# Mamba layer with routed experts on one core: expert tiles every 3.25 steps instead of 3.5, token gathers from step 197 and 4.5 steps apart, one product with C moved back to GpSimd

## The chip, the core and the metric

The kernel runs on one core of a Trainium2 chip. The metric is the time of one execution on the device, in microseconds. A core has five engines that run side by side, each through its own list of instructions in order: PE (TensorE, matmuls), DVE (VectorE), ACT (ScalarE), POOL (GpSimd) and SP (SyncE, here the queue from which nearly all DMAs are issued). They wait for one another by semaphores only. An instruction that waits holds back all that stands behind it on its engine.

## What is computed

The input is x of 8 batches x 512 tokens x 128. Each token is normalized; the result goes into two branches whose outputs are added to x. One branch is a bidirectional Mamba layer (a forward and a backward pass), the other a mixture of 8 experts of which each token takes the one with the highest router logit. Cut to what matters:

```
xn = layernorm(x)
# Mamba, once forward and once on the reversed sequence, per batch
xz = layernorm(xn)*g+b  @ in_w.T ; xi, z = split(xz)         # 256 channels each
xi = silu(conv4(xi) + conv_b)
dt, B, C = split(xi @ x_w.T)                                 # 8, 16, 16
delta = softplus(dt @ dt_w.T + dt_b) ; A = -exp(A_log)
h_t = h_{t-1} * exp(delta_t * A) + (delta_t * xi_t) * B_t    # 256 channels x 16 states
y_t = sum over states of h_t * C_t                           # "the product with C", then the sum
y = (y + xi * D) * silu(z) ; out = y @ out_w.T
attn = concat(out_f, out_b) @ combine_w.T + combine_b + xn
# experts
e = argmax(xn @ router_w.T)
ffn = (silu(xn @ gate_w[e].T) * (xn @ up_w[e].T)) @ down_w[e].T
result = x + attn + ffn
```

## The kernel before

**Units and steps.** A unit is one batch in one direction, so there are 16. One unit has 256 channels x 16 states x 512 tokens, cut into 16 steps of 128 rows x 1024 (two states of 32 channels). The whole kernel is a loop over 256 such steps, m = 0 to 255 (`LAST` = 256), written out on every engine: each engine's program runs `for m in range(STEPS)` and puts down, at each m, what is due there by tables and small functions of m.

**What a step is.** PE spreads delta*xi over the state rows for a pair of steps (`spread_du`, L600, put down at odd m for the pair m+1, m+2; it waits for the scan of step m-2, since the PSUM tile `in_b` has two halves). DVE multiplies by B (`du_B`, L1195, both steps of the pair), then scans (`scan`, L1212 or L1214). ACT makes the decays dA two steps ahead (L1002). POOL multiplies the scanned states `hs` by C, in place (L1435, 128x1024). Some of these products are done by DVE instead (`times_C`, L1221): those whose step stands in `C_ON_DVE`. PE then sums the states into the PSUM tile `y` (`sum_states`, L634).

**The ring of `hs`.** `hs` has NH = 13 buffers. Steps 8g to 8g+7 are a group; its even steps are summed at PE's step 8g+12 and its odd ones at 8g+13. The scan of step m needs the sum of the group and parity of step m-13. So the scan of step 8g+13 waits for the first sum of group g, and that waits for POOL's product of step 8g+6.

**Fronts.** The projections of the next unit (`in_proj` L561, `x_proj` L584, `dt_proj` L593, `z_proj` L575, and what ACT makes of them) stand some 16 to 4 steps ahead of it, in a ping-pong of PE and ACT over one PSUM bank. POOL makes delta and delta*xi (L1376, L1381), twice for each unit.

**Experts.** The routing sorts the tokens by expert into 39 tiles of 128 (`NTILE`). Tile n starts at step F0 + 7n//2 (`tiles_at`, F0 = 56): its loads stand there, gate matmuls (L784) 8 steps later, down and up matmuls (L802, L807) 10 steps later, ACT's SiLU and copies (L1066, L1071, L1088, L1090, L1094, L1098, with table loads L1011) 9 and 11 steps later, POOL's product gate*up (L1425) 11 or 12. Expert outputs go to HBM.

**Gathers.** When all tiles are out, the outputs are gathered back into token order, a batch at a time, in the order 0, 1, 2, 3, 6, 4, 5, 7 (`gather_step`, from step G0 = 206, 4 steps apart). At gather step + 2 POOL issues four indirect DMAs (L1408, or L1411 for the last two batches), ahead of the product with C of that step. For batches 0 to 5 PE adds them to the attention output at gather step + 7 (`final_mm`, L702 and, behind a wait for the gather, L704), ACT copies the sum (L1116), SP stores it. Batches 6 and 7 are added elsewhere (`experts_mm`, L691, at steps 236 and 257). At steps 233 to 237 PE also makes the output of batch 6 (L678, L685, L710). At step `FOUR` = 244 the preparation of the last sum begins (L643, L649).

Steps of the units' fronts, of the outputs and of the end (`front_step`, `out_step`, `LAST`) are fixed; the tables decide only the order of instructions on each engine.

## Time and profile before

| | before |
|---|---|
| runs, us | 912.49, 917.79, 912.06; median 912.49 |
| profiled execution, us | 918.05, of which the span is 916.1 |
| PE, DVE, ACT, POOL busy | 81%, 96%, 76%, 87% of the span |
| granted TensorE clock, mean | 0.886 of full speed |
| chain that ended last | POOL 15%, issue 9%, PE 5%, ACT 4%, DVE 1% |

The span is from the first to the last instruction of the profiled execution. Busy time of an engine is the time in which it executes something. An idle time is put down to the engine and line that ended it.
### The profile page before, as it was taken

How to read it: one execution, taken by the hardware profiler on the slowest of the kernel's cores; microseconds unless marked ns; L12 is line 12 of the kernel's file. 1: busy time of each engine (PE TensorE's matmuls, PEld its weight loads, DVE VectorE, ACT ScalarE, POOL GpSimd, SP SyncE). 2: the span in 40 equal slices, each digit the busy share in tenths (PEclk: the TensorE clock that was granted, in tenths of full speed). 3: DMA queues.
4: the chain of work that ended last, by engine and by line, in shares of the span. 5: the costliest groups of instructions: out<-in, count | busy, mean ns of one | idle time of the engine just before them, and what ended most of it. 6: DMA issues, size and time to landing. Idle time of an engine off the chain costs nothing. (4 is left out here: it accounts for less than half of the span.)

```text
span 916.1 us, 10763 instructions
## 1 busy us (share of the span) xinstructions
PE 743.8 (81%) x3045; PEld 331.8 (36%) x3045; DVE 882.0 (96%) x633; ACT 696.9 (76%) x1185; POOL 801.0 (87%) x450
## 2 busy tenths in 40 slices
PE   8889866877489978889798987989979879788376
PEld 4434321331034534354443533435333432223022
DVE  5999999999899999999899999999999999999987
ACT  4898965746379889888889889997979976575540
POOL 1578787999999999898898988999798999999995
PEclk9969889787799989989799998989999897979689
DMA  7795443235355555645455636555553534553300
GB/s 216 200 287 122 129 103 103 87 101 136 92 140 178 134 188 146 189 106 127 156 130 178 158 78 195 139 167 148 174 141 99 141 87 153 118 173 73 91 0 12
DMA packets 87371, 123.52 MB, mean 135 GB/s; under 512 B 7945, under 2 KB 58634, under 8 KB 83346
## 3 DMA queue, kind: packets, MB, share of 16 engines
q1 hardware_dynamic: 85266, 118.65, 46.9%
q0 software_dynamic: 2048, 4.20, 1.5%
q8 instruction: 25, 0.41, 0.2%
q14 instruction: 32, 0.26, 0.1%
HBM read 75.50 MB, written 14.29 MB: 98 GB/s over the span
## 5 line engine op out<-in xcount | busy, mean ns | idle before, releaser
L1435 POOL TENSOR_TENSOR hs<-hs,C_rep 128x1024 f32<-128x1024 f32 x250 | 585.7, 2362 | 46.7 <-DVE hs L1214 26.1
L1002 ACT ACTIVATE dA<-delta_rep,A_sb 128x511 f32<-128x511 f32 x512 | 335.4, 717 | 22.8 <-DMA delta_rep<-tmpA 18.6
L1195 DVE TENSOR_TENSOR in_b<-in_b,B_rep 128x1024 f32<-128x1024 f32 x256 | 300.2, 1217 | 12.2 <-PE in_b L600 10.5
L1214 DVE TENSOR_TENSOR_SCAN hs<-dA,in_b 128x1024 f32<-128x1024 f32 x128 | 285.5, 2269 | 5.1 <-PE y L634 5.1
L1212 DVE TENSOR_TENSOR_SCAN hs<-dA,in_b 128x1024 f32<-128x1024 f32 x128 | 285.3, 2269 | 1.0 <-PE y L634 1.0
L600 PE MATMUL in_b<-du,cst 128*128 128x512 f32 x256 | 159.1, 707 | 68.5 <-DVE hs L1214 49.6
L634 PE MATMUL y<-hs,cst 128*32 128x512 f32 x1016 | 136.3, 655 | 22.3 <-POOL hs L1435 22.3
L561 PE MATMUL front<-xpad,w_in 128*128 128x512 f32 x248 | 117.6, 609 | 8.5 <-ACT xi L931 6.4
L1011 ACT ACT_TABLE_LOAD x71 | 91.1, 1283 | 11.6 <-PE moe L784 7.1
L600 PEld LDWEIGHTS in_b<-du,cst 128*128 128x128 f32 x256 | 47.5, 216 | 142.7 <-issue 139.8
L561 PEld LDWEIGHTS front<-xpad,w_in 128*128 128x128 f32 x248 | 46.1, 195 | 64.0 <-issue 48.7
L634 PEld LDWEIGHTS y<-hs,cst 128*32 128x32 f32 x1016 | 28.3, 116 | 105.1 <-issue 67.2
L575 PE MATMUL front<-xpad,w_in 128*128 128x512 f32 x62 | 45.6, 828 | 17.1 <-ACT tmpB L967 11.5
L1376 POOL TENSOR_TENSOR tmpA<-tmpA,tmpB 128x512 f32<-128x512 f32 x31 | 39.5, 1273 | 13.7 <-ACT tmpB L977 13.7
L593 PE MATMUL front<-tmpB,w_dt 8*128 8x512 f32 x62 | 41.3, 750 | 9.2 <-ACT tmpB L953 7.1
L625 PE MATMUL y<-xi,diag_D 128*128 128x512 f32 x62 | 42.4, 772 | 7.8 <-ACT yg L985 6.5
L784 PEld LDWEIGHTS moe<-xsT,gu_w 128*128 128x128 f32 x234 | 33.0, 203 | 36.1 <-issue 36.1
L784 PE MATMUL moe<-xsT,gu_w 128*128 128x128 f32 x234 | 36.1, 294 | 9.7 <-ACT ys L1071 7.2
L1418 POOL TENSOR_TENSOR yg<-yg,zs 128x512 f32<-128x512 f32 x28 | 35.6, 1270 | 9.5 <-ACT yg L985 9.4
L802 PEld LDWEIGHTS moe<-dn_w,th_f 128*128 128x128 f32 x234 | 33.2, 202 | 26.3 <-issue 19.2
L584 PE MATMUL front<-xi,w_x 128*40 128x512 f32 x64 | 35.5, 683 | 7.9 <-ACT xi L944 7.9
L1381 POOL TENSOR_TENSOR du<-tmpA,xi 128x512 f32<-128x512 f32 x31 | 39.5, 1273 | 2.4
(158 smaller groups left out, 813.7 us busy)
## 6 DMA issues: line engine op xcount, KB each, us to landing
delta_rep<-tmpA SPq DMA_DIRECT2D x126, 256.0 KB, 3.9
C_rep<-dbc_scratch SPq DMA_DIRECT2D x16, 1024.0 KB, 7.1
B_rep<-dbc_scratch SPq DMA_DIRECT2D x15, 1024.0 KB, 5.1
gu_w<-in_gate_up SPq DMA_DIRECT2D x39, 384.0 KB, 3.7
dn_w<-in_down SPq DMA_DIRECT2D x39, 192.0 KB, 2.6
xs<-sorted_tokens SPq DMA_DIRECT2D x39, 64.0 KB, 3.8
sorted_ffn<-ys SPq DMA_DIRECT2D x39, 64.0 KB, 2.5
sorted_tokens<-up_f SPq DMA_DIRECT2D x9, 256.0 KB, 4.6
```

Source lines behind the costliest of these rows:

```text
L561: i = e.matmul((M if v == 0 and h else F)[:, :], w_in[:, d, k, h * P:(h + 1) * P], xpad[:, at:at + L], start=(k == 0), stop=(k == NTAP - 1))
L575: e.matmul((M if v == 0 and h else F)[:, :], w_in[:, d, NTAP, h * P:(h + 1) * P], xpad[:, 3:3 + L], start=True, stop=True).then_inc(pe_z, 1)
L600: e.matmul(in_b[:, 2 + 2 * (j % 2), :], spread(j), du[:, du_slot(v, j // 4), :], start=True, stop=True).then_inc(pe_du, 1)
L625: e.matmul(Y[:, :], diag_D[:, 2 * (u % 2) + h, :], xi[:, u % 2, h, :], start=True, stop=False, skip_group_check=True).then_inc(pe_skip, 1)
L634: i = e.matmul(Y[c * DD:(c + 1) * DD, :], sel, hs[:, (m + 2 * c + rh) % NH, r * L:(r + 1) * L], start=False, stop=(rh == 1 and r == RH - 1 ...
L784: i = e.matmul(M[:, c * P:(c + 1) * P], gu_w[:, w, 0, c * P:(c + 1) * P], xsT[:, n % 2, :], start=True, stop=True)
L1002: i = e.activation(dA[:, m % NA, r * L + 1:(r + 1) * L], src, ACT.Exp, scale=A_sb[:, d, 2 * p + jj, RH * rh + r:RH * rh + r + 1])
L1011: e.preload_act_table_set(name)
L1195: e.tensor_tensor(to, in_b[:, 2 + 2 * odd, :].unsqueeze(1).broadcast_to([P, RH, L]), by, ALU.mult).then_inc(dve_mult, 1)
L1212: e.tensor_tensor_scan(to, a[:, 0:n], b, 0.0, ALU.mult, ALU.add).then_inc(dve_scan, 1)
L1214: e.tensor_tensor_scan(to[:, ::-1], a[:, 1:n + 1][:, ::-1], b[:, ::-1], 0.0, ALU.mult, ALU.add).then_inc(dve_scan, 1)
L1435: e.tensor_tensor(hs[:, m % NH, :], hs[:, m % NH, :], C_rep[:, u % 2, RH * rh:RH * rh + RH, :].rearrange("p r t -> p (r t)"), ALU.mult).th ...
```

## The change

Three sets of numbers change and no instruction is new.

- Tile n starts at F0 + 13n//4, so every 3.25 steps. The last tile's start moves from step 189 to 179, its last copy on ACT from 207 to 197.
- The first gather step is 197 and they are 4.5 steps apart: 197, 201, 206, 210, 215, 219, 224, 228 in place of 206, 210, 214, 218, 222, 226, 230, 234. POOL's issues are two steps later each, at 199, 203, 208, 212, 217, 221, 226, 230. `FOUR` is still 244, written in another way.
- The product with C of step 180 is POOL's again. Steps 41, 56, 217, 226 and 255 stay with DVE.

```diff
-C_ON_DVE = (41, 56, 180, 217, 226, LAST - 1)
+C_ON_DVE = (41, 56, 217, 226, LAST - 1)
...
-G0 = F0 + 7 * NTILE // 2 + 14
+G0 = F0 + 13 * NTILE // 4 + 15
...
-    return [n for n in range(NTILE + more) if F0 + 7 * n // 2 + k == m]
+    return [n for n in range(NTILE + more) if F0 + 13 * n // 4 + k == m]
...
-    return G0 + 4 * GATHER_ORDER.index(b)
+    return G0 + 9 * GATHER_ORDER.index(b) // 2
```

**DVE, step 180** (L1195 multiplies by B, L1214 scans, L1221 is the product with C). This is the only difference on DVE:

```order
 L1195 TENSOR_TENSOR in_b<-in_b,B_rep 128x2x512
 L1214 SCALAR_TENSOR_TENSOR hs<-dA,in_b 128x1024 x2
-L1221 TENSOR_TENSOR hs<-hs,C_rep 128x1024
 L1195 TENSOR_TENSOR in_b<-in_b,B_rep 128x1024 x2
 L1214 SCALAR_TENSOR_TENSOR hs<-dA,in_b 128x1024 x2
```

One product has gone, between the scans of steps 180 and 181 and the products with B of steps 182 and 183.

**POOL, the last gathers.** L1435 is the product with C, L1418 a gate of the unit's output, L1376 and L1381 delta and delta*xi, L1408 and L1411 the four gathers of a batch. Before, from the gather of batch 4 (step 228) to that of batch 7 (step 236):

```order
L1408 DMA gu_w<-sorted_ffn,pos_u 128x128 x4
L1435 TENSOR_TENSOR hs<-hs,C_rep 128x1024 x2
L1418 TENSOR_TENSOR yg<-yg,zs 128x512
L1435 TENSOR_TENSOR hs<-hs,C_rep 128x1024 x2
L1408 DMA gu_w<-sorted_ffn,pos_u 128x128 x4
L1376 TENSOR_TENSOR tmpA<-tmpA,tmpB 128x512
L1381 TENSOR_TENSOR du<-tmpA,xi 128x512
L1435 TENSOR_TENSOR hs<-hs,C_rep 128x1024 x2
L1376 TENSOR_TENSOR tmpA<-tmpA,tmpB 128x512
L1381 TENSOR_TENSOR du<-tmpA,xi 128x512
L1435 TENSOR_TENSOR hs<-hs,C_rep 128x1024 x2
L1411 DMA attn_in<-sorted_ffn,pos_u 128x128 x4
```

After the change, from the gather of batch 4 (step 221) to the product of step 233:

```order
L1408 DMA gu_w<-sorted_ffn,pos_u 128x128 x4
L1435 TENSOR_TENSOR hs<-hs,C_rep 128x1024
L1418 TENSOR_TENSOR yg<-yg,zs 128x512
L1435 TENSOR_TENSOR hs<-hs,C_rep 128x1024 x4
L1408 DMA gu_w<-sorted_ffn,pos_u 128x128 x4
L1435 TENSOR_TENSOR hs<-hs,C_rep 128x1024 x3
L1411 DMA attn_in<-sorted_ffn,pos_u 128x128 x4
L1418 TENSOR_TENSOR yg<-yg,zs 128x512
L1435 TENSOR_TENSOR hs<-hs,C_rep 128x1024 x2
L1376 TENSOR_TENSOR tmpA<-tmpA,tmpB 128x512
L1381 TENSOR_TENSOR du<-tmpA,xi 128x512
L1435 TENSOR_TENSOR hs<-hs,C_rep 128x1024 x2
```

All gathers stand ahead of the product of step 230 now, where batch 5's and batch 7's used to stand behind it. The two deltas of the last unit keep their steps, 232 and 234.

**PE, steps 224 to 229.** L561 is `in_proj` of the last unit, L600 `spread_du`, L702 and L704 `final_mm`, L634 the sum over states, L584 `x_proj`. Before:

```order
L561 MATMUL front<-xpad,w_in 128x512 x4
L600 MATMUL in_b<-du,cst 128x512
L702 MATMUL moe<-attn_in,cst 128x512
L704 MATMUL moe<-gu_w,cst 128x512
L561 MATMUL front<-xpad,w_in 128x512 x4
L600 MATMUL in_b<-du,cst 128x512
L634 MATMUL y<-hs,cst 32x512 x8
```

After the change:

```order
L561 MATMUL front<-xpad,w_in 128x512 x4
L600 MATMUL in_b<-du,cst 128x512
L561 MATMUL front<-xpad,w_in 128x512 x2
L702 MATMUL moe<-attn_in,cst 128x512
L704 MATMUL moe<-gu_w,cst 128x512
L561 MATMUL front<-xpad,w_in 128x512 x2
L600 MATMUL in_b<-du,cst 128x512
L634 MATMUL y<-hs,cst 32x512 x8
```

The final product that stands here is batch 4's (step 226), seven steps after its gather step 219; before it was batch 3's (step 225). Behind it stand two matmuls of `in_proj` and the spread for steps 228 and 229. The final product of batch 5 moves from step 237 to 231.

## Rows read from the trace of the kernel before

**Rows 1.** The page, busy time of each engine (share of the span, instructions).
```profile
PE 743.8 (81%) x3045; PEld 331.8 (36%) x3045; DVE 882.0 (96%) x633; ACT 696.9 (76%) x1185; POOL 801.0 (87%) x450
```

**Rows 2.** Groups by line, DVE: count | busy us, mean ns | idle before, ended by.
```profile
L1195 DVE TENSOR_TENSOR in_b<-in_b,B_rep 128x1024 f32<-128x1024 f32 x256 | 300.2, 1217 | 12.2 <-PE in_b L600 10.5 <-DMA B_rep<-dbc_scratch 1.6
L1214 DVE TENSOR_TENSOR_SCAN hs<-dA,in_b 128x1024 f32<-128x1024 f32 x128 | 285.5, 2269 | 5.1 <-PE y L634 5.1
L1221 DVE TENSOR_TENSOR hs<-hs,C_rep 128x1024 f32<-128x1024 f32 x6 | 9.2, 1529 | 0.1
```

**Rows 3.** Waits of DVE: us in total, times, longest us.
```profile
DVE in_b L1195 <- PE in_b L600: 10.5, 7, 3.7
DVE hs L1214 <- PE y L634: 5.1, 2, 2.8
```

**Rows 4.** Timeline of DVE, steps 207 and 238 to 246.
```profile
737.56 2.26 DVE L1212 TENSOR_TENSOR_SCAN hs<-dA,in_b 128x1024 f32<-128x1024 f32 x1
...
844.63 4.46 DVE L1212 TENSOR_TENSOR_SCAN hs<-dA,in_b 128x1024 f32<-128x1024 f32 x2 [0.89 <-PE y L634]
...
855.63 2.34 DVE L1195 TENSOR_TENSOR in_b<-in_b,B_rep 128x1024 f32<-128x1024 f32 x2
...
862.25 2.34 DVE L1195 TENSOR_TENSOR in_b<-in_b,B_rep 128x1024 f32<-128x1024 f32 x2
...
869.04 2.29 DVE L1214 TENSOR_TENSOR_SCAN hs<-dA,in_b 128x1024 f32<-128x1024 f32 x1 [2.27 <-PE y L634]
875.02 2.36 DVE L1195 TENSOR_TENSOR in_b<-in_b,B_rep 128x1024 f32<-128x1024 f32 x2 [3.69 <-PE in_b L600]
```

**Rows 5.** Timeline of POOL, the first gather and the end of the last.
```profile
742.54 1.01 POOL L1408 DMA_INDIRECT gu_w<-sorted_ffn,pos_u  x1 [0.16 <-issue]
...
747.33 9.29 POOL L1435 TENSOR_TENSOR hs<-hs,C_rep 128x1024 f32<-128x1024 f32 x4
...
837.76 1.28 POOL L1376 TENSOR_TENSOR tmpA<-tmpA,tmpB 128x512 f32<-128x512 f32 x1
...
862.95 18.52 POOL L1435 TENSOR_TENSOR hs<-hs,C_rep 128x1024 f32<-128x1024 f32 x8
```

**Rows 6.** Timeline of PE, steps 224 to 245.
```profile
789.36 3.60 PE L561 MATMUL front<-xpad,w_in 128*128 128x512 f32 x8
...
838.18 1.95 PE L710 MATMUL front<-w_out,yg 128*128 128x128 f32 x16
...
842.64 1.92 PE L634 MATMUL y<-hs,cst 128*32 128x512 f32 x16
...
855.86 2.04 PE L600 MATMUL in_b<-du,cst 128*128 128x512 f32 x2 [5.52 <-DVE hs L1214]
865.33 3.64 PE L634 MATMUL y<-hs,cst 128*32 128x512 f32 x16 [7.43 <-POOL hs L1435]
```

**Rows 7.** The line of the gathers, issue to landing.
```profile
DMA to landing us min/median/max: 2.5/2.6/3.8
```

**Rows 8.** Timeline of DVE at two of its products with C.
```profile
174.93 3.05 DVE L1221 TENSOR_TENSOR hs<-hs,C_rep 128x1024 f32<-128x1024 f32 x1
...
652.58 1.20 DVE L1221 TENSOR_TENSOR hs<-hs,C_rep 128x1024 f32<-128x1024 f32 x1
```

**Rows 9.** Timeline of POOL beside these two.
```profile
174.53 2.36 POOL L1435 TENSOR_TENSOR hs<-hs,C_rep 128x1024 f32<-128x1024 f32 x1
...
652.75 3.26 POOL L1435 TENSOR_TENSOR hs<-hs,C_rep 128x1024 f32<-128x1024 f32 x1 [4.10 <-DVE hs L1214]
```

**Rows 10.** Timeline of DVE, first and last of four waits among the tiles.
```profile
342.89 2.36 DVE L1195 TENSOR_TENSOR in_b<-in_b,B_rep 128x1024 f32<-128x1024 f32 x2 [0.83 <-PE in_b L600]
...
539.96 2.36 DVE L1195 TENSOR_TENSOR in_b<-in_b,B_rep 128x1024 f32<-128x1024 f32 x2 [1.50 <-PE in_b L600]
```

**Rows 11.** Windows: us, PE, PEld, DVE, ACT, POOL busy, clock, DMA share, GB/s.
```profile
275.00:545.00 270.00, 236.54 (x1117) 118.97 (x1109) 264.50 (x161) 238.89 (x411) 249.52 (x137) 0.92 0.53 148
...
735.00:840.00 105.00, 83.91 (x265) 30.37 (x264) 104.97 (x65) 70.15 (x111) 97.11 (x63) 0.87 0.43 118
```

More of the change, by code:

```diff
@@ L105, in out_step @@
     return s0 + (8, 9, 18, 21, 4, 22, 25, 17)[k]
-FOUR = gather_step(GATHER_ORDER[-1]) + 10
+FOUR = LAST - 12
 STEPS = max(LAST + 6, out_step(NB - 1, 6) + 1, gather_step(NB - 1) + 10)
```

## The prediction, made before the changed kernel ran

> **What bounds the kernel now.** I read the busy times first: DVE is busy for 96% of the span, no other engine for more than 87% [rows 1]. Then DVE's groups: 256 products with B take 300.2 us, the 128 scans of L1214 285.5 us and those of L1212, 128 too, as much; that is 871 of its 882 us, and ahead of them it hardly waits [rows 2]. So the time is the steps of DVE, plus what DVE waits. A pair of steps takes 862.25 - 855.63 = 6.62 us where nothing disturbs it [rows 4], 3.31 a step. What can be gained is DVE's own work and its waits. These I took from the list of waits and looked up in the timeline: 10.5 us for the spread of PE and 5.1 us for PE's sums at L1214 [rows 3].
>
> They fall into two places. Four waits for the spread, 5.35 us together, lie among the expert tiles, the first of 0.83 us at 342.89 and the last of 1.50 us at 539.96 [rows 10]. Three lie at the end, ahead of steps 238, 245 and 246: 0.89 + 2.27 + 3.69 = 6.85 us [rows 4].
>
> The end is POOL's doing. The product of step 207 ends at 742.54 - 0.16 = 742.38, which is 2.56 us after its scan (737.56 + 2.26 = 739.82) [rows 4, 5]. The product of step 238 ends at 862.95 + 2.32 = 865.27, 18.4 us after its scan (846.90). I call this distance the lag. PE stands ready and starts the sum at 865.33, after 7.43 us of waiting for POOL [rows 6]. By the ring of 13 buffers the scan of step 245 needs that sum, and the spread for step 246 stands behind it, so DVE goes on at 875.02 only, 9.7 us after POOL's product.
>
> POOL's own prices: a product with C 18.52 / 8 = 2.32 us, the four gathers of a batch 747.33 - 742.38 = 4.95 us, a delta, a delta*xi or a gate (all 128x512) 1.28 us [rows 5]. From step 208 to 238 it has 29 products, 8 gathers, 8 deltas and 4 gates: 67.3 + 39.6 + 10.2 + 5.1 = 122.2 us; the trace has 122.9. In that time DVE needs 31 steps and two products, some 105 us. That is how the lag grows.
>
> **The change, part by part.**
>
> *Product of step 180.* DVE loses one instruction of 1.20 us at 652.58 [rows 8], 1.1 us without the overlap with the next. POOL gets it where it had idled for 4.10 us (ahead of 652.75) [rows 9], so it costs POOL nothing that shows. If that cover were gone, the lag would be 2.3 us longer there, against some 18 that the ring bears. **-1.1 us.** The row beside it shows more: POOL's product that started 0.17 us after DVE's took 3.26 instead of 2.36 us [rows 9], and DVE's product at 174.93, which started 0.40 us after one of POOL's, took 3.05 instead of 1.20 us [rows 8]. The Trainium skill says this (SBUF — State Buffer, Who interferes with whom): a VectorE instruction with both inputs in SBUF and a GpSimd one that reads SBUF exclude each other, whoever starts first has the port to its end. By that rule POOL pays 2.35 - 0.9 = 1.4 us for the product that it gets back; the trace agrees, with 0.9 us.
>
> *The gathers.* They start 9 steps earlier, so the lag starts to grow from step 199. I add the jobs up, e(m) being the end of scan m:
> - To product 221: 22 products, 6 gathers, 8 deltas, 2 gates: 51.0 + 29.7 + 10.2 + 2.6 = 93.5 us. DVE from e(198) to e(221): 11 pairs, 2.19 and one product, 76.1 us. Lag 2.5 + 17.4 = 19.9, and 0.6 more if this sum is short by as much as that of before: 20.5 us.
> - To product 230: 69.6 + 39.6 + 10.2 + 5.1 = 124.5 against 16 pairs and two products, 108.2. Lag 19.6 us.
> - To product 238: 88.2 + 39.6 + 15.4 + 6.4 = 149.6 against 134.7. Lag 18.3 us.
>
> So the lag at step 238, which made the waits of before, goes from 19.3 (18.4 without DVE's 0.89 us wait) to 18.3 only, and it is near 20 from step 221 on. Two new places come under it:
> - *Steps 226 to 228.* The last gather of batch 4 is issued about 1.0 us before the product of step 221 starts and lands 2.6 us later [rows 7]: e(221) + 20.5 - 2.35 - 1.0 + 2.6 = e(221) + 19.8. PE's final product of batch 4 waits for it, and behind it stand half of `in_proj` and the spread for step 228. DVE wants that at e(221) + 19.9 + 1.1 = 21.0. In PE's fast rows (a 128x512 matmul 0.45 us a pass, 3.60 / 8) the chain takes 0.9 + 1.8 + 0.9 = 3.6 us, in slow ones (2.04 for x2) 7.5 us [rows 6]. It is late by 2.4 or 6.3 us.
> - *Steps 236 to 238.* The sum that needs product 230 starts at e(230) + 19.6. Behind it stand the batch 6 experts' product, two output products and the spread for step 238, due at 22.05. Fast: 1.92 + 0.9 + 1.95 + 0.9 = 5.7, late by 3.2. Slow: 3.64 + 2.0 + 3.9 + 2.0 = 11.5, late by 9.1.
> - *Steps 244 to 246*, as before: 18.3 + 9.7 - 22.05 = 5.9 us late at the pace of before, 1.1 at twice that pace.
>
> Late amounts don't add: each wait of DVE lets POOL catch up by as much. What counts is the largest. Checked on before: 19.3 + 9.7 - 22.05 = 6.9 us, and the trace has 6.85. So the end costs between 3.2 and 9.1 us. The granted clock there was 0.87 up to 840, and the sum after 7.43 us of waiting ran at half speed, 3.64 instead of 1.92 us [rows 6, 11]. The new waits are as long (PE could take batch 4's final product some 11 us before its gather lands), so I take the slow end: 8.5 us. Against 6.85: **+1.65 us.** It is not a gain because the same 40 us of gathers go through POOL within steps that leave it less than 1 us a step.
>
> *Tiles every 3.25 steps.* The same 39 tiles, closer by 3.5 / 3.25 = 1.077 and over 10 steps earlier. In 275 to 545 PE is busy for 236.5 and ACT for 238.9 of 270 us [rows 11]; a wait of DVE comes where a tile's work falls among the front's ping-pong of PE and ACT. The four waits make 5.35 us. In proportion they become 5.8: **+0.4 us**, with both ends open: none at all (-5.35) or twice as much (+5.35), since their places are reshuffled. The cover of the first gather (its tiles stored in time) keeps its distance of two steps.
>
> **The sum**, against the profiled execution: 918.05 - 1.1 + 1.65 + 0.4 = 919.0 us. The median of the runs is 912.49, 5.56 below the profiled one, so I expect **913.4 us**, about the same.
>
> **The rivals.**
> - *The waits at the end shrink.* If PE stays fast, the end costs 3.2 instead of 6.85 us: 913.4 - (8.5 - 3.2) = 908.1. For it: nearly all of PE's rows around 790 to 843 are fast. Against it: the waits grow longer, and 865.33 was slow after one.
> - *The product's price alone shows.* The end and the tiles stay as they are: 912.49 - 1.1 = 911.4. For it: two of the three terms are small against their bounds.
> - *Tiles collide.* The waits among the tiles double: 913.4 + 5.0 = 918.4.
> - *DVE's products wait for POOL.* Before, the products of steps 217 and 226 met POOL at gathers. With a lag of 15 to 20 us POOL is never idle there, and each may meet one of POOL's products. As at 174.93, each is then 1.85 us longer [rows 8, 9]; I let this vanish in the waits that follow, but if it came on top it would be 913.4 + 3.7 = 917.1. This is the port rule of the page named above turned against the change.
> - *Slower by more than 1%: the waits add up.* PE has 21 us of idle time in the 105 us up to 840 [rows 11] and must now wait for the gathers of batches 1 to 5 as well, with the front of the last units behind. If it can't catch up between two waits, the three late amounts add: 6.3 + 9.1 + 5.9 = 21.3 instead of 6.85, less the 1.65 already counted: 913.4 + 12.8 = 926.2. It decides from a total of 16.7 us of DVE waits at the end on (6.85 + 9.1 + 1.1 - 0.4), where 912.49 is passed by 1%.
>
> **How the numbers follow.** Forecast 0.48 (own range 911 to 917), shrinking waits 0.24, product alone 0.08, tiles 0.08, port 0.06, adding waits 0.06. The range runs from the shrunken waits, 908, to the tiles' collision with a slower end, 920. A measurement of this kernel can tell about 1% (9 us) from no change. More than 9 us faster would need the end's and the tiles' waits all gone as well as the product (13.3 us in all); I give it 0.02. Slower by over 1% is the last rival and a little of two others: 0.07. The rest is 0.91.
>
> **What the profile after would show.** Right: DVE's L1221 five times; POOL's first gather near 712 us; POOL's lag near 20 us from step 221 to 236; PE waiting for gathers at L704 (no such wait before); DVE's waits at the end ahead of steps 228, 238 and 246, 5 to 9 us together; among the tiles 4 to 8 us. Wrong: if POOL's lag stays below 16 us, my prices for it are; if DVE waits less than 4 us at the end, PE's pace is; if the waits exceed 16 us, that they relieve each other is; if L1221 has rows near 3 us at steps 217 and 226, the port matters.

## The result: 2.5% slower, and the profile after

| | before | after |
|---|---|---|
| runs | median 913.3 us (6 runs, 912.06 to 917.79) | median 936.83 us (6 runs, 936.08 to 939.48) |
| ratio of the medians | | 1.0249, interval 1.022 to 1.0277 |
| profiled execution | 918.05 us, span 916.1 | 937.19 us, span 935.2 |
| granted clock, mean | 0.886 | 0.885 |
| DVE's idle time among the tiles (250 to 715 us) | 5.6 us | 18.3 us |
| DVE's products with C at steps 217 and 226 | 1.22 + 1.20 us | 10.67 + 2.56 us |
| DVE's idle time at the end of the loop | 6.85 us | 2.8 us |

I had forecast 913.4 us, within 908 to 920. The change is slower by 23.5 us in the medians, which is outside the range and on the other side of the 1% bound.

DVE is busy for 892.9 us, 11 more than before [rows 1], though it has one instruction less. These are the engines' busy times and the products with B on the page of the kernel after:

```profile
PE 749.7 (80%) x3045; PEld 337.9 (36%) x3045; DVE 892.9 (95%) x632; ACT 697.0 (75%) x1185; POOL 803.3 (86%) x451
L1195 DVE TENSOR_TENSOR in_b<-in_b,B_rep 128x1024 f32<-128x1024 f32 x256 | 300.1, 1217 | 15.9 <-PE in_b L600 15.7
```

The products with B take what they took before [rows 2], and so do the scans. The added busy time is in the line of DVE's products with C (count, shortest / median / longest in ns), where the longest was about 3 us before [rows 8]:

```profile
L1221 DVE TENSOR_TENSOR hs<-hs,C_rep x5: 1197/2561/10666, 174.0 to 927.3; 128x1024 f32<-128x1024 f32 x5
```

DVE's timeline after shows where it is (start, length, ..., in brackets the idle time ahead). The product of step 217 takes 10.67 us and that of step 226 2.56:

```profile
785.22 10.67 DVE L1221 TENSOR_TENSOR hs<-hs,C_rep 128x1024 f32<-128x1024 f32 x1
...
828.91 2.56 DVE L1221 TENSOR_TENSOR hs<-hs,C_rep 128x1024 f32<-128x1024 f32 x1
...
863.94 2.29 DVE L1212 TENSOR_TENSOR_SCAN hs<-dA,in_b 128x1024 f32<-128x1024 f32 x1 [1.37 <-PE y L634]
...
867.61 2.36 DVE L1195 TENSOR_TENSOR in_b<-in_b,B_rep 128x1024 f32<-128x1024 f32 x2 [1.38 <-PE in_b L600]
```

The last two rows are all that DVE waits at the end, 2.75 us. POOL's timeline over the same time says what stands beside the long product:

```profile
781.97 4.67 POOL L1435 TENSOR_TENSOR hs<-hs,C_rep 128x1024 f32<-128x1024 f32 x2
786.59 1.27 POOL L1418 TENSOR_TENSOR yg<-yg,zs 128x512 f32<-128x512 f32 x1
787.81 6.98 POOL L1435 TENSOR_TENSOR hs<-hs,C_rep 128x1024 f32<-128x1024 f32 x3
794.95 1.79 POOL L1411 DMA_INDIRECT xn<-sorted_ffn,pos_u  x1 [0.16 <-issue]
```

When DVE's product starts at 785.22, POOL is in the second of two products. It goes on with a gate and three more, each right behind the one before. They end at 787.81 + 6.98 = 794.79. DVE's product ends at 785.22 + 10.67 = 795.89, 1.10 us later, which is its own length. So it lasted 9.4 us longer than its work because POOL left no gap. It is counted as busy. Beside the length of its row, only the chain that ended last shows it, with no engine as its cause:

```profile
785.36 10.45 issue
```

The waits of DVE after, in 250 to 715 us (us in total, times, longest):

```profile
DVE in_b L1195 <- PE in_b L600: 11.6, 10, 2.9
DVE hs L1212 <- PE y L634: 4.7, 3, 2.2
DVE hs L1212 <- ACT dA L1002: 0.9, 1, 0.9
DVE hs L1214 <- ACT dA L1002: 0.6, 2, 0.3
DVE hs L1214 <- PE y L634: 0.5, 1, 0.5
```

That is 18.3 us in 17 waits. Before there were four waits of 5.35 us for the spread [rows 10] and one of 0.2 us for PE's sums, 5.6 us. Several of the runs below have the same program up to 715 us, but for the product of step 180, so their profiled executions say how much such a total moves from one execution to the next. Before's tables of tiles are in e3, e8 and e11 too: 3.7, 5.1 and 3.5 us. The changed tables are in e1, e2 and e4 too: 14.9, 24.8 and 19.9 us. The two groups stay well apart, but one total is good to some 5 us either way.

**The account between the two profiled executions:** tiles 18.3 - 5.6 = +12.7; the two products 13.23 - 2.42 = +10.8; the end of the loop 2.8 - 6.85 = -4.05; the product of step 180 -1.1. The sum is +18.4 us, and 937.19 - 918.05 = +19.1 us was measured. Between the medians the difference is 4.4 us larger, because the profiled execution of before lies 4.75 us above the median of its runs and that of after 0.4 us above its own.

### The profile page after: what moved, and what is told of

Same layout as the page of the kernel before. It is cut to its first block and busy times, and to the rows that moved or that the text cites. A ratio compares the mean times of both kernels' runs of the same rounds, so it can differ in the third digit from the quotient of the medians.

```text
span 935.2 us, 10763 instructions
## 1 busy us (share of the span) xinstructions
PE 749.7 (80%) x3045; PEld 337.9 (36%) x3045; DVE 892.9 (95%) x632; ACT 697.0 (75%) x1185; POOL 803.3 (86%) x451
## 5 line engine op out<-in xcount | busy, mean ns | idle before, releaser
L1435 POOL TENSOR_TENSOR hs<-hs,C_rep 128x1024 f32<-128x1024 f32 x251 | 587.4, 2359 | 58.2 <-DVE hs L1214 39.6
L1195 DVE TENSOR_TENSOR in_b<-in_b,B_rep 128x1024 f32<-128x1024 f32 x256 | 300.1, 1217 | 15.9 <-PE in_b L600 15.7
L1214 DVE TENSOR_TENSOR_SCAN hs<-dA,in_b 128x1024 f32<-128x1024 f32 x128 | 285.7, 2270 | 4.2 <-PE y L634 3.6
L600 PE MATMUL in_b<-du,cst 128*128 128x512 f32 x256 | 156.1, 695 | 70.2 <-DVE hs L1214 45.3
L634 PE MATMUL y<-hs,cst 128*32 128x512 f32 x1016 | 137.7, 661 | 17.3 <-POOL hs L1435 17.3
L561 PE MATMUL front<-xpad,w_in 128*128 128x512 f32 x248 | 121.4, 624 | 9.3 <-ACT xi L931 7.2
L600 PEld LDWEIGHTS in_b<-du,cst 128*128 128x128 f32 x256 | 47.5, 215 | 145.0 <-issue 145.0
L561 PEld LDWEIGHTS front<-xpad,w_in 128*128 128x128 f32 x248 | 47.2, 200 | 66.8 <-issue 51.0
L634 PEld LDWEIGHTS y<-hs,cst 128*32 128x32 f32 x1016 | 28.6, 117 | 99.4 <-issue 68.1
L575 PE MATMUL front<-xpad,w_in 128*128 128x512 f32 x62 | 45.3, 822 | 18.7 <-ACT zs L937 11.4
L784 PE MATMUL moe<-xsT,gu_w 128*128 128x128 f32 x234 | 38.7, 308 | 20.1 <-ACT ys L1071 14.0
L1376 POOL TENSOR_TENSOR tmpA<-tmpA,tmpB 128x512 f32<-128x512 f32 x31 | 39.6, 1276 | 17.3 <-ACT tmpB L977 17.2
L784 PEld LDWEIGHTS moe<-xsT,gu_w 128*128 128x128 f32 x234 | 34.1, 213 | 46.4 <-issue 46.3
L593 PE MATMUL front<-tmpB,w_dt 8*128 8x512 f32 x62 | 39.4, 718 | 8.7 <-ACT tmpB L953 4.5
L1418 POOL TENSOR_TENSOR yg<-yg,zs 128x512 f32<-128x512 f32 x28 | 35.6, 1272 | 11.9 <-ACT yg L985 11.8
L802 PEld LDWEIGHTS moe<-dn_w,th_f 128*128 128x128 f32 x234 | 33.1, 203 | 33.5 <-issue 24.2
L802 PE MATMUL moe<-dn_w,th_f 128*128 128x128 f32 x234 | 36.1, 294 | 7.5 <-POOL th_f L1425 5.3
L1381 POOL TENSOR_TENSOR du<-tmpA,xi 128x512 f32<-128x512 f32 x31 | 39.5, 1273 | 2.4
```

The costliest lines, as they stand in the source:

```text
L561: i = e.matmul((M if v == 0 and h else F)[:, :], w_in[:, d, k, h * P:(h + 1) * P], xpad[:, at:at + L], start=(k == 0), stop=(k == NTAP - 1))
L575: e.matmul((M if v == 0 and h else F)[:, :], w_in[:, d, NTAP, h * P:(h + 1) * P], xpad[:, 3:3 + L], start=True, stop=True).then_inc(pe_z, 1)
L600: e.matmul(in_b[:, 2 + 2 * (j % 2), :], spread(j), du[:, du_slot(v, j // 4), :], start=True, stop=True).then_inc(pe_du, 1)
L634: i = e.matmul(Y[c * DD:(c + 1) * DD, :], sel, hs[:, (m + 2 * c + rh) % NH, r * L:(r + 1) * L], start=False, stop=(rh == 1 and r == RH - 1 ...
L784: i = e.matmul(M[:, c * P:(c + 1) * P], gu_w[:, w, 0, c * P:(c + 1) * P], xsT[:, n % 2, :], start=True, stop=True)
L802: i = e.matmul(M[:, IFP:IFP + H], th_f[:, (n - 2) % 3, c * P:(c + 1) * P], dn_w[:, (n - 2) % ND, c, :], start=(c == 0), stop=(c == NCH - 1))
```

## The experiments

The kernel before was run again beside each group of experiments. Its medians were 911.86 us beside e1 to e4, 912.86 beside e5 to e8, 913.52 beside e9 and e10, and 914.02 beside e11. Two things need a cause: the 12.7 us among the tiles, and the long product.

### e1: the tiles alone

The kernel before with the tiles every 3.25 steps. Gathers and products stay.

```diff
-    return [n for n in range(NTILE + more) if F0 + 7 * n // 2 + k == m]
+    return [n for n in range(NTILE + more) if F0 + 13 * n // 4 + k == m]
```

> The kernel before with only the tile spacing changed: expert tiles every 3.25 steps; gathers stay at 206 and 4 steps apart, DVE keeps the product of step 180. In the changed kernel's trace DVE's waits between 270 and 705 us are 17.7 us, in the trace before 5.5. Theory tiles (the closer tiles alone make these waits): the same waits of 15 to 20 us here, and 10 to 15 us more than before in all, ratio 1.011 to 1.016; no DVE product with C longer than 1.3 us at step 217. Rival (the waits among the tiles come with the removed product of step 180 or with something else of the change): waits of 4 to 8 us, ratio within 0.997 to 1.004.

Measured: median 930.61 us (925.58 to 933.62), ratio 1.021, interval 1.0157 to 1.0262. The tiles alone bring 18.75 us in the medians, most of the change's 23.5. What is left, some 5 us, is for the gathers and the product of step 180 together; neither was run alone, and the intervals of the two ratios overlap. DVE's product of step 217 took 1.22 us here, so the gathers are needed for the long one. DVE's waits in 250 to 715 us, profiled execution of 925.58 us:

```profile
DVE in_b L1195 <- PE in_b L600: 9.6, 10, 2.2
DVE hs L1212 <- PE y L634: 3.2, 3, 2.6
```

With the three small groups (0.9 + 0.6 + 0.6) that is 14.9 us, 9.3 more than before. One wait followed back shows how they come about. First ACT's timeline in e1:

```profile
493.72 1.28 ACT L1011 ACT_TABLE_LOAD   x1
495.01 2.56 ACT L1002 ACTIVATE dA<-delta_rep,A_sb 128x511 f32<-128x511 f32 x4
...
498.88 0.28 ACT L1071 COPY ys<-moe 128x128 f32<-128x128 f32 x1
```

and then PE's:

```profile
499.41 0.91 PE L784 MATMUL moe<-xsT,gu_w 128*128 128x128 f32 x6 [3.63 <-ACT ys L1071]
...
502.18 2.08 PE L625 MATMUL y<-xi,diag_D 128*128 128x512 f32 x2
...
505.82 1.81 PE L600 MATMUL in_b<-du,cst 128*128 128x512 f32 x2
```

ACT copies the tile's output (`ys`) behind a table load, four exponentials and three more instructions. PE, whose next instruction is the tile's product, stands for 3.63 us. It comes back at half speed: 2.08 us for a 128x512 matmul of two passes, where the last one ahead of the wait took 1.02 (granted clock 1.00 in 495 to 499.4 us, 0.59 in 499.4 to 507.7). So the spread for the next step ends at 507.63, and DVE waits 0.71 us for it:

```profile
507.67 2.36 DVE L1195 TENSOR_TENSOR in_b<-in_b,B_rep 128x1024 f32<-128x1024 f32 x2 [0.71 <-PE in_b L600]
```

PE waited for this copy (L784 for L1071) ten times between 250 and 715 us, 13.7 us; before, seven times and 7.2 us. Its waits for weight loads went from 2.5 to 6.2 us and those for POOL's product for the tile (L802 for L1425) from none to 6.7 us.

### e2: the two products on POOL

The changed kernel with DVE's products of steps 217 and 226 given to POOL.

```diff
-C_ON_DVE = (41, 56, 217, 226, LAST - 1)
+C_ON_DVE = (41, 56, LAST - 1)
```

> The changed kernel, with DVE's products of steps 217 and 226 given to POOL too. In the changed kernel they take 10.67 and 2.56 us instead of 1.2. Theory port (DVE's product can't start while POOL runs products back to back, and waits until POOL issues a gather): both rows are gone and DVE runs on at 217, 13 us less there; but POOL has 4.7 us more work and isn't relieved by that wait, so its lag, which was 10.8 us at step 221, goes to 22 or more, and DVE waits at PE's sums and spreads from step 228 on for 9 to 16 us instead of 2.8. In all -6 to +1 us against the changed kernel: 931 to 938 us. Rival (the 10.67 us were a wait of that place in the program, for memory or for data, which any instruction there would have had): the next instruction, the product with B of step 218, is late by 9 us instead, and POOL's lag stays near 11 us.

Measured: median 938.34 us (933.04 to 942.83), ratio 1.0267, interval 1.0197 to 1.0338. This can't be told from the changed kernel. The long product is gone, and the lag comes in its place: product 221 ends 23.0 us behind its scan. DVE's waits in 715 to 930 us:

```profile
DVE in_b L1195 <- issue: 7.3, 1, 7.3
DVE in_b L1195 <- PE in_b L600: 5.6, 2, 4.1
```

With 0.3 us more for ACT that is 13.2 us instead of 2.8. The wait of 7.3 us, for which the profile names no one, lies ahead of step 234 (DVE goes on at 857.09). In PE's timeline the spread that it needs ends at 855.67 + 1.38 = 857.05, and ahead of that spread PE waits 7.43 us for the gather of batch 5 and comes back slow:

```profile
847.53 2.07 PE L704 MATMUL moe<-gu_w,cst 128*128 128x512 f32 x2 [7.43 <-DMA gu_w<-sorted_ffn,pos_u]
...
855.67 1.38 PE L600 MATMUL in_b<-du,cst 128*128 128x512 f32 x2
```

So the two products held DVE for 10.8 us longer than their work and saved 10.4 us of waits, because POOL caught up in the meantime: the standing by itself is hardly a net loss against giving the products to POOL. (The waits among the tiles, 24.8 us here, are the spread between executions named above.)

### e3: a DVE product beside a run of POOL's

The kernel before with one more product on DVE, at step 242, where POOL has products in a row and no gather.

```diff
-C_ON_DVE = (41, 56, 180, 217, 226, LAST - 1)
+C_ON_DVE = (41, 56, 180, 217, 226, 242, LAST - 1)
```

> The kernel before, with the product of step 242 given to DVE as well, in a stretch without gathers, where POOL runs products back to back (from 857 us on). Theory port: DVE's product starts near 862 us and ends only when POOL falls idle, which it does once it has made the products of 238 to 241 and 243 and must wait for the scan of step 244, near 875 us: a row of 10 to 14 us. The waits of 2.3 and 3.7 us at steps 245 and 246 vanish into it, so the kernel is 4 to 8 us slower than before. Rival (a DVE product waits for one POOL product at most, as at 174.93 in the trace before: 3.05 us): a row of 1.2 to 3.5 us, and the time within 3 us of before or below it, as POOL has one product less.

Measured: median 924.59 us (two runs, 922.88 and 926.29), ratio 1.0126, interval 1.0058 to 1.0195. DVE's row for it:

```profile
859.86 13.36 DVE L1221 TENSOR_TENSOR hs<-hs,C_rep 128x1024 f32<-128x1024 f32 x1
```

and POOL's:

```profile
859.32 1.27 POOL L1418 TENSOR_TENSOR yg<-yg,zs 128x512 f32<-128x512 f32 x1
860.54 11.60 POOL L1435 TENSOR_TENSOR hs<-hs,C_rep 128x1024 f32<-128x1024 f32 x5
877.76 4.66 POOL L1435 TENSOR_TENSOR hs<-hs,C_rep 128x1024 f32<-128x1024 f32 x2 [5.62 <-DVE hs L1214]
```

The product stands behind the rest of a gate and five products, six instructions of POOL. POOL goes idle at 872.14, and DVE's product ends at 873.22, 1.08 us later. That is 12.1 us of standing, and nothing but a gap on POOL ends it: a gather after the change, idleness here. DVE's waits of before at steps 245 and 246 (2.27 + 3.69 us [rows 4]) are gone, since POOL caught up. The kernel is made slower all the same: by 4.8 us between the profiled executions, within the 4 to 8 us expected, but by 12.7 us between the medians, which of two runs is a rough figure and outside it.

### e4: the two products at POOL's gathers

The changed kernel with DVE's products at steps 215 and 225, where by the lag POOL is issuing gathers.

```diff
-C_ON_DVE = (41, 56, 217, 226, LAST - 1)
+C_ON_DVE = (41, 56, 215, 225, LAST - 1)
```

> The changed kernel, with DVE's two products at steps 215 and 225 instead of 217 and 226, where POOL should be issuing the gathers of batches 3 and 4. Theory port: POOL issues gathers while DVE makes the product of 215, so that row is 1.2 to 1.5 us and the one of 225, at the edge of a gather, 1.2 to 3.5; POOL's lag at step 221 is 19 to 21 us instead of 10.8; DVE waits 4 to 9 us at the end instead of 2.8. In all 5 to 9 us less than the changed kernel: 928 to 932 us. Rival (long rows come with any product of DVE in that stretch): a row of 5 us or more again and 936 us.

Measured: median 932.02 us (928.25 to 936.98), ratio 1.0211, interval 1.0144 to 1.0277. DVE's timeline:

```profile
779.89 1.23 DVE L1221 TENSOR_TENSOR hs<-hs,C_rep 128x1024 f32<-128x1024 f32 x1
...
814.25 1.23 DVE L1221 TENSOR_TENSOR hs<-hs,C_rep 128x1024 f32<-128x1024 f32 x1
816.96 2.36 DVE L1195 TENSOR_TENSOR in_b<-in_b,B_rep 128x1024 f32<-128x1024 f32 x2 [1.48 <-PE in_b L600]
...
824.11 2.36 DVE L1195 TENSOR_TENSOR in_b<-in_b,B_rep 128x1024 f32<-128x1024 f32 x2 [0.43 <-PE in_b L600]
...
849.56 2.36 DVE L1195 TENSOR_TENSOR in_b<-in_b,B_rep 128x1024 f32<-128x1024 f32 x2 [5.49 <-PE in_b L600]
```

Against the changed kernel that is 4.8 us less, at the edge of the 5 to 9 us expected, and the intervals of the two ratios overlap. Between the profiled executions it is 4.8 us too: the two products give back 10.8 us, the waits at the end take 4.6 and those among the tiles 1.6.

Both products take 1.23 us, two steps and one step away from where they took 10.67 and 2.56. POOL pays for the second one with a gather that takes 1.75 instead of 0.95 us:

```profile
814.54 1.75 POOL L1408 DMA_INDIRECT gu_w<-sorted_ffn,pos_u  x1 [0.30 <-issue]
...
818.81 2.35 POOL L1435 TENSOR_TENSOR hs<-hs,C_rep 128x1024 f32<-128x1024 f32 x1
```

This last row is the product of step 221. It ends at 821.16, 20.2 us after its scan (which ends at 800.99); 20.5 us was forecast. PE's timeline has the two final products that wait for their gathers and then delay DVE, batch 4's and batch 5's:

```profile
820.37 1.12 PE L704 MATMUL moe<-gu_w,cst 128*128 128x512 f32 x2 [0.69 <-DMA gu_w<-sorted_ffn,pos_u]
...
840.11 2.07 PE L704 MATMUL moe<-gu_w,cst 128*128 128x512 f32 x2 [5.73 <-DMA gu_w<-sorted_ffn,pos_u]
```

Batch 4's starts at 820.37, where the prediction's sum gives 800.99 + 19.8 = 820.8. PE was fast, DVE had waited 1.48 us already at step 226, and what is left ahead of step 228 is 0.43 us. Batch 5's is a place that I hadn't reckoned: it makes the wait of 5.49 us ahead of step 234. Its gather took 6.78 us to land, in the chain that ended last:

```profile
833.28 6.78 DMA gu_w<-sorted_ffn,pos_u
```

where all gathers of before landed within 3.8 us [rows 7]. Of the stretch in which it was under way and of the one behind it the windows say this (us, busy PE, PEld, DVE, ACT, POOL, clock, DMA share, GB/s):

```profile
833.00:840.00 7.00, 1.38 (x4) 0.31 (x2) 7.00 (x6) 2.11 (x4) 6.71 (x4) 0.89 0.84 296
840.00:850.00 10.00, 9.70 (x12) 3.05 (x12) 4.51 (x3) 6.77 (x13) 8.91 (x8) 0.56 0.23 68
```

The DMA engines were busy for 84% of those 7 us; with the earlier gathers batch 5's now falls beside the broadcasts of B and C for the last unit. That these delay it is argued from the window, no run took them away. Behind PE's wait the clock is 0.56, near the lower of its levels, 0.5, and the matmul of two passes takes 2.07 us in place of 1.12. Together DVE waits 7.4 us at the end, where the prediction had 8.5 for the changed kernel.

### e5, e6, e7: the same tiles at other places

The kernel before; only the table of tile steps is changed. e5: 3.5 steps, all one step later. e6: 3.25 steps, one step later. e7: 3.5 steps with the gaps in the order 4, 3 in place of 3, 4. The gathers stay where they were.

```diff
 # e5 (e6: the same, and 13 * n // 4 in place of 7 * n // 2 for the tiles)
-F0 = R0 + 29
-G0 = F0 + 7 * NTILE // 2 + 14
+F0 = R0 + 30
+G0 = R0 + 29 + 7 * NTILE // 2 + 14
```

```diff
 # e7
-    return [n for n in range(NTILE + more) if F0 + 7 * n // 2 + k == m]
+    return [n for n in range(NTILE + more) if F0 + (7 * n + 1) // 2 + k == m]
```

> The kernel before with all expert tiles one step later, still every 3.5 steps; gathers as before. DVE's waits between 250 and 715 us are 5.5 us before and 14.9 us with tiles every 3.25 steps (e1_tiles). Theory density (more of the gaps between tiles are 3 steps, where PE's gate matmuls stand in the same step as ACT's copy that they wait for; 28 of 38 gaps at 3.25, 19 at 3.5): the shift changes nothing of it, waits of 4 to 8 us, time within 4 us of before. Theory place (what counts is where tiles fall within the 16 steps of a unit's front): waits move by 4 us or more, to 9 to 16 us, and the time goes up by 4 to 12 us.

> The kernel before with tiles every 3.25 steps and all of them one step later. Theory density: as e1_tiles, waits of 13 to 17 us among the tiles, 925 to 932 us. Theory place: waits differ from the 14.9 us of e1_tiles by 4 us or more, either way.

> The kernel before with tiles every 3.5 steps, but the gaps of 3 and 4 steps swapped: 4 from an even tile to the odd one behind it, 3 to the next even one. The number of gaps of 3 is as before (18 of 38). POOL's product of an even tile stands 11 steps behind the start of the odd tile, and PE's down matmuls of it 10 steps behind the start of the next even one: 2 steps instead of 3. Theory pool_product (PE's waits for POOL's product gate*up, 0 before and 5 to 7 us in the two kernels with 3.25, are a main part of the loss): these waits appear here, 5 us or more, and DVE's waits among the tiles go to 10 us or more. Theory density: DVE's waits 4 to 8 us, PE waits for POOL's product 3 us at most.

(Of the 38 gaps between tiles 29 are of three steps at 3.25, and 19 at 3.5, in e7 too; the texts above give 28 and 18.)

| tiles | median, us | ratio, interval | DVE's waits 250 to 715 us |
|---|---|---|---|
| before: 3.5 | 912.86 | | 5.6 |
| e5: 3.5, a step later | 930.86 | 1.0189, 1.0157 to 1.0221 | 16.7 |
| e7: 3.5, gaps swapped | 939.62 | 1.0293, 1.0273 to 1.0314 | 20.5 |
| e1: 3.25 | 930.61 | 1.021, 1.0157 to 1.0262 | 14.9 |
| e6: 3.25, a step later | 932.78 | 1.0221, 1.0198 to 1.0244 | 19.7 |

Density alone doesn't explain the loss: at 3.5 steps, a step later, the kernel is as slow as at 3.25 (e5's 18 us are more than the 4 to 12 that its own theory of place had). With the same gaps in another order it is the slowest of all. The tiles of the kernel before stand in a good place, and any of the four other tables costs 18 to 27 us. The last column is one execution for each table and can't rank the four slow ones: 14.9 to 24.8 us were seen with e1's table alone. The waits that open on PE differ from table to table. The largest group of PE's in e5, e6 and e7, each in 250 to 715 us:

```profile
PE moe L784 <- ACT ys L1071: 10.5, 8, 2.5
PE moe L784 <- DMA gu_w<-in_gate_up: 9.3, 5, 4.2
```

```profile
PE moe L784 <- ACT ys L1071: 26.8, 15, 4.6
```

```profile
PE moe L784 <- ACT ys L1071: 14.0, 7, 4.9
...
PE moe L802 <- POOL th_f L1425: 5.9, 4, 2.4
```

ACT's copy comes first in all three, with 10.5 to 26.8 us where before had 7.2. Next to it stand weight loads in e5 and POOL's product for the tile in e7, where the swap leaves it a step less. That product's wait came as e7's theory said, 5 us or more, but in e5 and e6 it is 1.4 and 1.5 us and the loss is there all the same, so it is no common cause.

### e9 and e10: less of ACT, less of PE

Both start from e1. Their expectations say what they leave out of the experts. e9 leaves out the tiles' SiLU and with it the change of ACT's function tables, 36 of 71 table loads. e10 keeps one of every three matmuls of the tiles' products.

```diff
 # e9
-                        table(SILU_SET)
-                        e.activation(th_f[:, n % 3, :], M[:, 0:IFP], ACT.Silu).then_inc(act_gate, 1)
+                        e.activation(th_f[:, n % 3, :], M[:, 0:IFP], ACT.Identity).then_inc(act_gate, 1)
...
-                        e.activation(t, t, ACT.Silu).then_inc(act_thf, 2)
+                        e.activation(t, t, ACT.Identity).then_inc(act_thf, 2)
```

```diff
 # e10
-                    for c in range(NCH):
+                    for c in range(1):
...
-                    for c in range(NCH if n >= 2 else 0):
+                    for c in range(1 if n >= 2 else 0):
...
-                    for c in range(NCH if n < NTILE else 0):
+                    for c in range(1 if n < NTILE else 0):
```

> The kernel with only the tiles every 3.25 steps (e1_tiles), with the SiLU of the expert tiles left out (a plain copy in its place), so that the tiles need no table loads on ACT: about 40 of its 71 loads of 1.28 us fall away, 1.3 us of some 3.1 us of ACT's work for a tile. The output of the experts is another. Theory ACT (PE is held up in its list by ACT's copies, which stand behind table loads and decays): DVE's waits between 250 and 715 us fall from 14.9 to below 5 us and PE's waits for ACT's copy ys fall from 13.7 to below 6 us; 908 to 918 us. Theory PE (the tiles' matmuls themselves leave PE no room): DVE's waits stay above 10 us.

> The same kernel (tiles every 3.25 steps) with one of three matmuls of each tile's gate, up and down products, so that PE has about 1.2 us of work for a tile instead of 3.1; ACT's work is as in e1_tiles. The output of the experts is another. Theory PE: DVE's waits between 250 and 715 us fall below 5 us. Theory ACT: they stay above 10 us, and PE waits longer for ACT's copies than in e1_tiles.

Measured: e9 918.54 us (915.91 to 924.38), ratio 1.0055, interval 1.0019 to 1.0091. e10 917.76 us (915.16 to 919.84), ratio 1.0049, interval 1.0018 to 1.0079. Against e1's 1.021 each gives back about three quarters of the loss, in the medians 5.0 and 4.2 us above before instead of 18.75. DVE's waits in 250 to 715 us came to 12.2 us in e9, in a profiled execution 4.4 us above its median, and to 5.9 us in e10. Neither came below the 5 us that its theory asked for. e10's are these:

```profile
DVE in_b L1195 <- PE in_b L600: 3.0, 3, 2.0
DVE hs L1212 <- PE y L634: 2.9, 2, 2.5
```

PE's wait for the copy did not shrink in e10:

```profile
PE moe L784 <- ACT ys L1071: 17.6, 10, 4.0
```

(In e9 it was 8.0 us.) So the loss doesn't belong to one engine. PE may stand for ACT for 17.6 us and still have the spread ready in time, if its own share of the tile is short. With the full share of PE, leaving out half of the table loads gives back nearly as much in the medians. Neither of the two theories, that it is ACT's table loads or that it is PE's share, holds alone. That what costs is the sum of both in one step, the wait for ACT and the work behind it, fits both runs and the wait followed in e1, but is argued from them.

### e8 and e11: what can be had from the kernel before

The kernel before with the product of step 180 back on POOL, as in the change, and one DVE product in the stretch in which POOL's lag is largest: at step 235, where POOL issues a gather (e8), and at 238 too (e11).

```diff
-C_ON_DVE = (41, 56, 180, 217, 226, LAST - 1)
+C_ON_DVE = (41, 56, 217, 226, 235, LAST - 1)
```

```diff
-C_ON_DVE = (41, 56, 180, 217, 226, LAST - 1)
+C_ON_DVE = (41, 56, 217, 226, 235, 238, LAST - 1)
```

> The kernel before, with the product of step 180 on POOL and that of step 235 on DVE instead, where POOL issues the gathers of batch 5 (832.8 to 837.8 us in the trace before, DVE's place is 834.9). Theory port: the row at step 235 is 1.2 to 1.5 us; POOL's lag at step 238 falls by some 3.4 us to 15 us, so the waits at the end go from 6.85 us to 2 to 4 us in the profile; at least 2 us less in all, 908 to 911 us, ratio 0.994 to 0.999. Rival (the waits at the end are PE's, not POOL's, in most runs): the same time within 1 us.

> The kernel e8_best with the product of step 238 on DVE too. Its place on DVE is at 845.3 us in the trace of e8_best, where POOL is in the product of step 235 until 846.3 us and then issues the gathers of batch 7. Theory port: the row takes 2.2 us (1.05 of waiting and 1.2). PE's first sum of the last full group but one, which waited for POOL's product of step 238 until 859.4 us, needs POOL only to step 236 and starts some 5 us earlier, so DVE's wait of 3.6 us ahead of step 246 is gone; the balance is 1 to 2 us less than e8_best, 906.5 to 908.5 us. Rival (in most runs e8_best has no wait at the end, so only the cost of the product is left): 1 to 2 us more than e8_best, 910 to 911 us.

Measured: e8 908.9 us (12 runs, 905.96 to 915.02) beside 912.86 of before (17 runs), ratio 0.9962, interval 0.994 to 0.9983. e11 910.9 us (12 runs, 907.84 to 915.02) beside 914.02, ratio 0.997, interval 0.9945 to 0.9994. Both are faster than the kernel before, by 3 to 4 us, and e8 is as fast as expected. e11 is not: 906.5 to 908.5 us was expected, and 910.9 is what its rival had. Which of the two is better these runs don't tell. DVE's timeline of e8:

```profile
830.86 1.22 DVE L1221 TENSOR_TENSOR hs<-hs,C_rep 128x1024 f32<-128x1024 f32 x1
...
869.03 2.36 DVE L1195 TENSOR_TENSOR in_b<-in_b,B_rep 128x1024 f32<-128x1024 f32 x2 [3.61 <-PE in_b L600]
```

The product takes no more than its own time, POOL's lag at step 238 is 16.2 instead of 18.4 us, and one wait of 3.61 us is left of 6.85. In e11 DVE's second product starts while POOL is in a single one with a gather behind it. DVE's row, then POOL's:

```profile
845.64 2.12 DVE L1221 TENSOR_TENSOR hs<-hs,C_rep 128x1024 f32<-128x1024 f32 x1
```

```profile
844.34 2.35 POOL L1435 TENSOR_TENSOR hs<-hs,C_rep 128x1024 f32<-128x1024 f32 x1
846.83 1.80 POOL L1411 DMA_INDIRECT attn_in<-sorted_ffn,pos_u  x1
```

It waits for that one to end at 846.69 and ends at 847.76: 2.12 us instead of 1.22. This is the kind of collision that the prediction had in mind, with 1.85 us. No wait at the end of the loop is left in e11, which saves the 3.61 us of e8, but the 0.9 us and the second product's own 1.1 us take 2.0 of them back. Between the profiled executions 1.4 us are left, and the medians don't show them.

## Why the prediction was wrong, step by step

**What bounds the kernel** held. DVE's steps take what they took, and all but 0.8 of the 19.1 us between the profiled executions lie in DVE's waits and its products. The reading that DVE's waits fall into two places left out 2.8 + 1.4 us ahead of 250 us; they are 3.1 + 1.3 us after, so nothing hangs on them.

**The product of step 180, -1.1 us.** Held, as far as the rows show. DVE has five products, and DVE waits nowhere between 639 and 677 us after the change; step 180 stands near 663 there. e8 contains it too, but no run has it alone.

**Tiles, +0.4 us: the step that failed.** It measured +12.7 us in the profiled execution and 18.75 us in the medians of e1. (It also moved POOL's first gather: 725.88 us, where "near 712 us" was to be seen.) Two things in it were wrong. The first is that I scaled the waits by the spacing: e5 and e7 have the old spacing and lose as much. What I called "reshuffled" was the whole effect. The kernel before is not an average case but a table whose tiles happen to fall, or were chosen to fall, well among the front's work; its 5.35 us say what this one table costs and nothing of its neighbours. The second is the upper bound. "Twice as much" was drawn from the waits. The row that should have widened it is PE's and ACT's occupation, 236.5 and 238.9 of 270 us [rows 11]: both are 88% busy, so there are some 30 us of slack in 82 steps, 0.4 us a step by this estimate, and a wait of 3.6 us in the wrong place uses up what several steps have. That this is why the waits grow is argued, not shown.

**DVE's products beside POOL, taken as nothing on top, rival price 1.85 us each: failed too, in size.** They stood for 10.8 us. The mechanism was named and the profile was to show rows "near 3 us" at steps 217 and 226; it shows 10.67 and 2.56. The price came from the row at 174.93, where POOL had one product and then a gap [rows 8, 9]. The Trainium skill (SBUF — State Buffer, Who interferes with whom) calls the port pair that VectorE shares with GpSimd "an exclusive lock", and says of VectorE's modes that use the whole pair that whoever issues first gets it "for the whole instruction". By that rule, taken over to this product, DVE's product would follow POOL's current instruction, within 2.4 us; e11's 2.12 us and the 2.56 us at step 226 agree. At step 217 and in e3 the measurement differs from it, and the measurement decides: DVE stood through five and six instructions of POOL, though its own was there before all but the first of them were started.

**The lag and the end of the loop, +1.65 us.** In the changed kernel this came out as -4.05, and the lag as 10.8 us at step 221, not 20.5. POOL went on working for the 9.4 us in which DVE stood. So the standing and the end belong together: +10.8 - 4.05 = +6.75 us, where the prediction had +1.65. Two of the tests named ahead thus say "wrong": the lag stays below 16, and DVE waits less than 4 us at the end. Their reasons don't hold, though. POOL's prices were right, as e4 shows, where nothing relieves POOL: 20.2 us of lag and 7.4 us of waits, against 20.5 and 8.5. That the size of the waits came out in e4 was partly luck. The place ahead of step 228 gave 0.43 instead of 2.4 to 6.3 us, and that ahead of step 238 nothing; 5.49 us came from batch 5's gather ahead of step 234. I had followed the gather of batch 4 only, and priced every landing at the 2.6 us of [rows 7].

**That waits relieve each other** held, in more than one form: e3 loses the waits of steps 245 and 246, and in e2 the removal of 10.8 us of standing brings 10.4 us of waits.

**The rivals.** "Tiles collide" was the right mechanism with a third of its price (5 us beside 12.7 to 18.75), and "DVE's products wait for POOL" the right one with a third of its own (3.7 beside 10.8). I gave them 0.08 and 0.06, and didn't put them together; at my prices both would have made 913.4 + 5.0 + 3.7 = 922.1 us, still 14.7 us short. "The waits add up" gave 926.2 by another way, which did not occur.

**The profiled execution and the median.** I took the offset of 5.56 us off the sum as a constant. It isn't one: after the change it is 0.4 us. In what the profiled execution of before differs from its median the traces don't say, since there is one trace of it.

**Open.** Which tile at which step makes the difference was not followed beyond single examples. e1's profiled execution was the lowest of its six; the tile term of 12.7 us is therefore of one execution each, and the 18.75 us of the medians is the better figure. Over the four profiled executions with either set of tables the mean waits are 19.5 and 4.5 us, 15.0 us apart. Of e7's 20.2 us between profiled executions, DVE's waits from 250 us to the end of the loop make 17.6; the rest was not placed.

## What to carry to other kernels

Where a schedule is laid out by hand and two engines pass work back and forth at near 90% each, as here, a shift of a table by one step is an experiment, not a detail: the waits that one placement shows give no price for another, and the control run is the old density shifted by a step. Place a VectorE instruction with two inputs in SBUF (the on-chip memory) by what GpSimd does at that moment, by its lag and not by its step: beside an indirect DMA or an idle time it costs its own 1.2 us, ahead of a run of products it costs the whole run, and it is shown as busy time. The product of step 180 moved to such a slot, where it shortens the lag, was worth 4 us here (e8).

## What the runs showed of the hardware

A VectorE product with both inputs in SBUF that finds GpSimd at work isn't served between GpSimd's instructions, as long as these follow each other without a gap. It stood for 9.4 us (after the change, five instructions) and 12.1 us (e3, six), and ran within 1.1 us of the first gap. A gap of 0.16 us ahead of an indirect DMA was enough. The indirect DMA itself doesn't hold such a product up: in e4 the one at 779.89 started 0.09 us into the issue of a gather and took 1.23 us. The other way round the issue of a gather beside such a product took up to 1.80 us instead of 0.94 to 1.00 (1.47 and 1.49 before, 1.79 and 1.80 after, 1.41 in e8), and in e4 beside the product at 779.89 still 0.94: a delay of one VectorE product at most.
